# Two chained cross-attentions on one core: block 0 of pass 2 reordered on all engines, layer 1's softmax maxima by groups of 8 heads, and the last block's second spread moved between its outputs

## The chip, the core and the metric

The kernel runs on one core of one Trainium2 chip. The metric is the device time in microseconds (us), lower is better. A core has TensorE (PE, matrix products), VectorE (DVE), ScalarE (ACT) and GpSimd (POOL); SyncE (SP) issues the DMAs. Matrix products write to 8 PSUM banks of 128 x 512 f32. POOL works on SBUF alone.

## The reference

x is 2 x 2048 x 512, the context 2 x 128 x 512, and the mask is over context positions. Two layers follow each other:

```
layer 0 (16 heads of 64):  A = exp(mask*(Q K') - max over all) * mask;  A /= sum(A) + 1e-15
                           y = layernorm((A V) Wo + bo + x) * gamma + beta
layer 1 (16 heads of 32):  A = softmax(Q K' / sqrt(32)), queries from y, keys and values from the context
                           out = layernorm((A V) Wo + bo + y) * gamma + beta
```

## The kernel before

The 4096 query rows are 8 blocks (`i`, `NB` = 8) of 512 rows; a block has 4 tiles (`n`) of 128 rows. Dense products are made of three products of high and low parts (`split_product`, lines 408 to 411), so there is a `*_hi` (ACT) and a `*_lo` (POOL or DVE) version of each operand. A "step" below is one chunk `c` of such a product: 3 matrix products of 128 x 512.

**Pass 1** makes layer 0's attention for all blocks and stores it unscaled (`u_dram`) with its row sums. Its end is `values0(NB - 1, j)`, j = 0 to 3, each behind `mask_probs` of DVE; two banks hold its results, which ACT copies out (`save_u`), so chunk c waits until chunk c - 2 is saved.

**Pass 2** runs blocks 0 to 7. Each engine has an order written out by hand, and semaphores (`wait_ge`) tie the engines. For block i:

- `attention0(i, n)` (POOL) scales `a_raw` by the reciprocal sums `r_bc`, which come back from DRAM (`store_r`, then `load_r`); for block 0 DVE does it (`attention_first`). `a0_high` (ACT) and `a0_low` (POOL) split it, and `output0(i, n)` (PE, 8 steps, `Z_BANKS[n % 2]`) multiplies it by Wo.
- `rows0`, `statistics0`, `moments0` (DVE), `scales0` (POOL, half a block) and `normal0` (ACT) are the layernorm; `transposes` (PE), `yt_high` (ACT), `yt_low` (DVE) give yt.
- `queries1(i, c)` (PE, 4 steps), `q1_high` (ACT), `q1_low` (DVE) and `logits1(i, c)` (PE, 4 heads, one per `L_BANKS`) follow; `scores_and_max1` (DVE, per head) copies the logits out and takes row maxima into `mx1`.
- **The maxima over rows.** `max_row1` (PE) transposes the maxima of a group of heads, `head_max` (DVE) reduces them, `max_spread1` (PE) sends the result to all partitions, `shift1` (DVE) turns it into the bias of `exponential1` (ACT, per head). A group is 4 heads, four groups to a block, in `MAX1_BANKS` (the two `Z_BANKS` and `L_BANKS[0]`). Groups 1 to 3 fall among the first two `output0` tiles of the next block.
- `sums1(i, c)`, `values1(i, c)` (PE), `divisors1` (DVE: `den1`, reciprocal, cast to `r1_hi`, `r1_split`), `spread1` (PE), `save_u1` (ACT), `attention1` (DVE), `a1_high` (ACT), `a1_low` (POOL) give layer 1's attention inside block i + 1; `output1`, `rows1`, `statistics1`, `moments1`, `scales1`, `normal1`, `out_scale`, `out_bias` the rest.

ACT at the start of block i + 1 has the remaining `exponential1(i, h)`, `normal0(i + 1, 0)`, `normal0(i + 1, 1)`, `a0_high(i + 2, 0)`, `save_u1`, `a0_high(i + 2, 1)`, `a1_high`. POOL there has `scales0(i + 1, 0)`, then `attention0` and `a0_low` of block i + 2 for tiles 0 and 1, then `a1_low(i, c)`, then `scales0(i + 1, 1)`.

**Block 0** prepares layer 1's weights too: PE's `value_product` for v1 and 32 small products for the bias bq1, DVE's `wq1_lo` and `wo1_lo`. On DVE `wo1_lo` stands ahead of `rows0(0, 3)` and waits for `r_stored` of all blocks, since its source lies where another buffer is being stored from. On POOL, `scales0(0, 1)` stands behind `attention0(1, 0)` and `attention0(1, 1)`.

**The last block** has no next one: `divisors1` is done in two halves, and for each half PE makes four `spread_last`, then two `output1` tiles. The half's `attention1`, `a1_high` and `a1_low` lie between the spreads and the outputs. DVE adds, normalizes and scales tiles 1 to 3 (`rows1`, `statistics1`, `moments1`, lines 1259 and 1263).

## Time and profile before

| what | value |
|---|---|
| median of 3 runs | 934.73 us (931.45 to 936.63) |
| the profiled execution's own time | 935.43 us |
| its span, first to last instruction | 933.6 us |
| mean granted TensorE clock | 0.972 of 2.4 GHz |
| busy: PE, DVE, ACT, POOL | 875.1, 552.8, 419.6, 454.2 us |
| pass 2 starts near | 387 us |
| one block of pass 2, from one block's first `sums1` to the next one's | 61.7 us |

The span is the time between the first and the last instruction; the run's own time has 1.8 us more. Busy time of PE counts modelled ends of pipelined products, so steps are read from start to start. A line such as L409 is a line of the program.

### The profile page before, as it was taken

Reading aid. Unit: us, or ns where it says so; the run is one execution under the profiler, and the core shown is the slowest. Engines: PE = TensorE matmul, PEld = TensorE weight load, DVE = VectorE, ACT = ScalarE, POOL = GpSimd, SP = SyncE. Lnnn points to the kernel's source line nnn. Section 1 sums busy time; section 2 is a strip of 40 time slices with the busy share of each in tenths; the row PEclk is TensorE's granted clock in tenths of the full one; section 3 lists DMA queues with packets and bytes.
Section 4 is the critical chain, followed back from the end, with each engine's and each line's share of the span. In section 5 each row is a group of like instructions: output and inputs, shape, how many; then the busy total and the mean of one; then the engine's idle time right before and its main releaser. Section 6 shows DMA issues by size and latency. Waiting matters only on the chain.

```text
span 933.6 us, 12121 instructions
## 1 busy us (share of the span) xinstructions
PE 875.1 (94%) x4556; PEld 588.2 (63%) x4556; DVE 552.8 (59%) x1080; ACT 419.6 (45%) x560; POOL 454.2 (49%) x284
## 2 busy tenths in 40 slices
PE   7989999999999989794999999999999999999964
PEld 6567466574756654473667687686776876767633
DVE  1357575665656577835666566555665665556645
ACT  2325374553536437323453644536545454363440
POOL 0510312303031113428388579586795786853714
PEclk9999999999999999896999999999999999999977
DMA  9622416152452426971341431523414224210011
GB/s 351 230 81 111 168 70 225 62 194 91 149 194 59 182 92 222 275 212 40 96 128 48 136 91 50 177 68 100 149 46 135 91 76 151 68 69 1 1 46 45
DMA packets 47641, 111.55 MB, mean 119 GB/s; under 512 B 4704, under 2 KB 8544, under 8 KB 47584
## 3 DMA queue, kind: packets, MB, share of 16 engines
q1 hardware_dynamic: 47584, 110.78, 35.9%
q8 instruction: 36, 0.59, 0.3%
q14 instruction: 21, 0.17, 0.1%
HBM read 76.69 MB, written 34.08 MB: 119 GB/s over the span
## 4 chain that ended last, share of the span: by engine, by line
PE 70%; DVE 11%; POOL 7%; DMA 4%; issue 4%; ACT 3%; SPq 1%; POOLq 0%; DVEq 0%
PE bank L409 15%; PE bank L411 14%; PE bank L410 14%; PE bank L457 6%; PE bank L469 6%; PE bank L450 5%; PE bank L616 2%; DVE den L1101 2%; PE bank L574 2%; DVE scores L1084 2%; PE bank L397 2%; POOL a_lo L1308 2%; POOL a_raw L1298 2%; PE bank L403 1%; POOL resid L1370 1%
## 5 line engine op out<-in xcount | busy, mean ns | idle before, releaser
L409 PE MATMUL bank<-wo_lo,a_hi 128*128 128x512 f32 x384 | 157.0, 409 | 10.8 <-POOL a_lo L1423 6.9
L1270 POOL TENSOR_TENSOR x_lo<-x_raw,x_hi 128x2048 fp32r<-128x2048 f32 x8 | 39.0, 4876 | 235.1 <-ACT x_hi L758 235.1
L411 PE MATMUL bank<-wo_hi,a_hi 128*128 128x512 f32 x384 | 151.6, 395 | 0.0
L410 PE MATMUL bank<-wo_hi,a_lo 128*128 128x512 f32 x384 | 151.6, 395 | 0.0
L970 DVE CUSTOM_DVE_ANT_0 scores<-bank,mask_f 128x512 f32<-128x512 f32 x128 | 80.8, 687 | 58.1 <-PE bank L450 58.1
L846 ACT ACTIVATE scores<-scores,sh 128x512 f32<-128x512 f32 x128 | 82.0, 712 | 56.3 <-DVE sh L1094 56.2
L409 PE MATMUL bank<-x_lo,wq_hi 128*128 128x512 f32 x256 | 103.0, 402 | 4.3 <-DVE q_lo L961 3.5
L1303 POOL TENSOR_TENSOR a_lo<-a_raw,a_hi 128x1024 fp32r<-128x1024 f32 x32 | 78.4, 2453 | 50.1 <-ACT a_hi L827 50.1
L411 PE MATMUL bank<-x_hi,wq_hi 128*128 128x512 f32 x256 | 100.6, 393 | 0.0
L410 PE MATMUL bank<-x_hi,wq_lo 128*128 128x512 f32 x256 | 100.6, 393 | 0.0
L768 ACT ACTIVATE q_hi<-bank,bq_sb 128x512 fp32r<-128x512 f32 x64 | 44.1, 689 | 116.8 <-PE bank L411 114.0
L409 PEld LDWEIGHTS bank<-wo_lo,a_hi 128*128 128x128 f32 x384 | 73.2, 191 | 35.9 <-issue 10.8
L1084 DVE TENSOR_SCALAR_CACHE_REDUCE scores<-bank 128x512 f32<-128x512 f32 x128 | 81.9, 680 | 6.3 <-PE bank L574 5.7
L411 PEld LDWEIGHTS bank<-wo_hi,a_hi 128*128 128x128 f32 x384 | 73.2, 191 | 16.1
L410 PEld LDWEIGHTS bank<-wo_hi,a_lo 128*128 128x128 f32 x384 | 73.4, 191 | 13.9
L994 DVE TENSOR_TENSOR scores<-scores,mask_f 128x2048 f32<-128x2048 f32 x32 | 77.2, 2416 | 0.0
L961 DVE SCALAR_TENSOR_TENSOR q_lo<-bank,bq_sb,q_hi 128x512 fp32r<-128x512 f32 x64 | 47.9, 749 | 49.1 <-ACT q_hi L768 48.6
L1298 POOL TENSOR_TENSOR a_raw<-a_raw,r_bc 128x1024 f32<-128x1024 f32 x28 | 69.5, 2481 | 11.3 <-DMA r_bc<-r_dram 11.3
L827 ACT ACTIVATE a_hi<-a_raw 128x1024 fp32r<-128x1024 f32 x32 | 33.9, 1060 | 77.1 <-POOL a_raw L1298 71.3
L469 PE MATMUL bank<-scores,v 128*64 128x512 f32 x256 | 63.7, 620 | 4.8 <-ACT u_out L790 4.7
L457 PE MATMUL bank<-scores,summer 128*32 128x512 f32 x512 | 67.0, 618 | 0.0
L774 ACT ACTIVATE scores<-scores,neg_mx 128x2048 f32<-128x2048 f32 x32 | 64.1, 2002 | 0.0
(134 smaller groups left out, 1602.4 us busy)
## 6 DMA issues: line engine op xcount, KB each, us to landing
u_dram<-u_out SPq DMA_DIRECT2D x8, 2048.0 KB, 7.4
a_raw<-u_dram SPq DMA_DIRECT2D x32, 512.0 KB, 3.6
r_bc<-r_dram SPq DMA_DIRECT2D x56, 256.0 KB, 4.9
x_raw<-x_t SPq DMA_DIRECT2D x8, 1024.0 KB, 5.5
xn<-x_n SPq DMA_DIRECT2D x8, 1024.0 KB, 5.1
xb_dram<-xn SPq DMA_DIRECT2D x8, 1024.0 KB, 5.2
z<-xb_dram SPq DMA_DIRECT2D x32, 256.0 KB, 2.8
out<-z SPq DMA_DIRECT2D x7, 1024.0 KB, 6.8
```

What stands on the lines that cost most here:

```text
L409: nc.tensor.matmul(dst, lh, rl, start=first, stop=False)
L410: nc.tensor.matmul(dst, ll, rh, start=False, stop=False)
L411: return nc.tensor.matmul(dst, lh, rh, start=False, stop=last)
L457: last = nc.tensor.matmul(dst[32 * g:32 * g + 32, :], summer[:, j, :], scores[:, G * j + g, :], start=(j == 0), stop=(j == HG - 1))
L469: last = nc.tensor.matmul(U_BANKS[c % 2][a * DK0:(a + 1) * DK0, :], v0[:, b, h * DK0:(h + 1) * DK0], scores[:, h, :], start=True, stop=True)
L774: nc.scalar.activation(four, four, ACT.Exp, bias=neg_mx[:]).then_inc(exp_ready, 1)
L846: nc.scalar.activation(scores[:, h, :], scores[:, h, :], ACT.Exp, bias=sh1[:, h:h + 1], scale=SCALE1).then_inc(probs1_ready, 1)
L970: nc.vector.tensor_tensor_reduce(out=scores[:, h, :], in0=L0_BANKS[h % 4][:], in1=mask_f[:], scale=1.0, scalar=-3e38, op0=ALU.mult, op1=AL ...
L994: nc.vector.tensor_tensor(four, four, mask_f[:].unsqueeze(1).to_broadcast([P, HG, QB]), ALU.mult).then_inc(probs_ready, 1)
L1084: nc.vector.tensor_scalar(scores[:, h, :], L_BANKS[h % HC1][:], 1.0, -3e38, ALU.mult, ALU.max, accum_out=mx1[:, h:h + 1]).then_inc(scores1 ...
L1298: nc.gpsimd.tensor_tensor(a_raw[:, n, :], a_raw[:, n, :], r_bc[:, n % 2, :], ALU.mult).then_inc(attn0_ready, 1)
L1303: nc.gpsimd.tensor_tensor(a_lo[:, n, :], a_raw[:, n, :], f(a_hi[:, n, :]), ALU.subtract).then_inc(a0_ready, 1)
```

## The change

**Maxima (blocks 0 to 6).** Two groups of 8 heads in place of four of 4, in `TQ_BANKS[0]`, which is free at that time, so that `output0` of the next block no longer waits for `shift1`:

```diff
-        MAX1_BANKS = [Z_BANKS[0], Z_BANKS[1], Z_BANKS[1], L_BANKS[0]]
+        MAX1_BANK = TQ_BANKS[0]
+        def max_groups(i):
+            return [(0, 8), (8, 16)] if i < NB - 1 else [(0, 8), (8, 12), (12, 16)]
...
+                    elif i == 1:
+                        pe.wait_ge(z0_ready, n + 3)
                     else:
-                        pe.wait_ge(shift1_ready, C1 * (i - 1) + (1 if n == 0 else 3))
+                        pe.wait_ge(z1_ready, QT * (i - 2) + n + 3)
...
+                if g == 0:
+                    pe.wait_ge(q1_ready, C1 * i + 3)
+                else:
+                    pe.wait_ge(shift1_ready, N_MAX * i + g)
+                pe.wait_ge(scores1_ready, H1 * i + last)
```

PE's order at the start of a block, and from `queries1(i, 2)` on:

```diff
             for i in range(NB):
                 before = i > 0
-                output0(i, 0, 0, C0 // 2)
+                output0(i, 0, C0 // 2 if before else 0)
+                output0(i, 1, 0, 1)
+                if before:
+                    logits1(i - 1, 3)
+                output0(i, 1, 1, 6)
+                if before:
+                    max_row1(i - 1, 1)
+                output0(i, 1, 6)
                 if before:
                     max_spread1(i - 1, 1)
-                    logits1(i - 1, 3)
-                    max_row1(i - 1, 2)
-                output0(i, 0, C0 // 2)
-                if before:
-                    max_spread1(i - 1, 2)
-                output0(i, 1, 0, C0 // 2)
-                if before:
-                    max_row1(i - 1, 3)
-                output0(i, 1, C0 // 2)
-                if before:
-                    max_spread1(i - 1, 3)
...
                 queries1(i, 2)
+                if i + 1 < NB:
+                    output0(i + 1, 0, 0, 1)
                 logits1(i, 1)
+                queries1(i, 3)
+                if i + 1 < NB:
+                    output0(i + 1, 0, 1, 2)
                 max_row1(i, 0)
-                queries1(i, 3)
+                if i + 1 < NB:
+                    output0(i + 1, 0, 2, 4)
                 max_spread1(i, 0)
                 logits1(i, 2)
-                max_row1(i, 1)
```

Behind the last spread `sums1` and `values1` now come as sums 0, 1, values 0, 1, sums 2, values 2, sums 3, values 3. ACT does 8 exponentials at the end of a block and 8 at the start of the next (before: 4 and 12). DVE:

```diff
                 if before:
-                    shift1(i - 1, 1)
-                    scores_and_max1(i - 1, H1 - 4)
-                    scores_and_max1(i - 1, H1 - 3)
-                    head_max(i - 1, 2)
-                    scores_and_max1(i - 1, H1 - 2)
-                    scores_and_max1(i - 1, H1 - 1)
-                    shift1(i - 1, 2)
+                    for h in heads(C1 - 1):
+                        scores_and_max1(i - 1, h)
                 rows0(i, 0)
                 statistics0(i, 0)
                 moments0(i, 0)
                 if before:
-                    head_max(i - 1, 3)
-                    shift1(i - 1, 3)
+                    head_max(i - 1, 1)
+                    shift1(i - 1, 1)
                 rows0(i, 1)
```

**Block 0.** PE: `value_product` for the first batch moves from behind `transposes(0, 1)` to behind `values0(NB - 1, 3)`; the 32 products for bq1 move from ahead of `transposes(0, 2)` to behind `transposes(0, 3)`; `queries1(0, 0)` waits for `wq1_lo` and no longer for `wo1_lo` and bq1. ACT, ahead of its loop:

```diff
-            for n in range(2):
-                save_u(NB - 1, 2 * n + 2, 2 * n + 4)
-                a0_high(0, n)
+            save_u(NB - 1, 2, 6)
+            a0_high(0, 0)
             save_u(NB - 1, 6)
+            a0_high(0, 1)
             a0_high(0, 2)
             a0_high(0, 3)
```

In ACT's block 0 `a0_high(1, 0)`, formerly behind `normal0(0, 1)`, comes behind `normal0(0, 3)`; `a0_high(1, 1)`, from there too, behind `yt_high(0, 3)`; `a0_high(1, 2)` and `a0_high(1, 3)` behind `q1_high(0, 1)` and `q1_high(0, 2)`. DVE: `k1_low(2)` and `k1_low(3)` move ahead of `attention_first(0)`; `wo1_lo` with its waits moves from ahead of `rows0(0, 3)` to behind `q1_low(0, 0)`; bq1's copy to behind `yt_low(0, 3)`. POOL:

```diff
                 scales0(i, 0)
+                if not before:
+                    scales0(i, 1)
                 if more:
                     for n in (0, 1):
                         attention0(i + 1, n)
```

**Last block.** Its maxima are three groups (8, 4 and 4 heads), with `sums1(7, 0)` and `sums1(7, 1)` among them, and:

```diff
-            for half in range(2):
-                for c in range(C1):
-                    spread_last(half, c)
-                output1(i, 2 * half)
-                output1(i, 2 * half + 1)
+            for c in range(C1):
+                spread_last(0, c)
+            output1(i, 0)
+            for c in range(C1):
+                spread_last(1, c)
+            for n in range(1, QT):
+                output1(i, n)
```

## Rows read from the trace of the kernel before

**Rows 1.** The page, busy time by engine.

```profile
PE 875.1 (94%) x4556; PEld 588.2 (63%) x4556; DVE 552.8 (59%) x1080; ACT 419.6 (45%) x560; POOL 454.2 (49%) x284
```

**Rows 2.** PE's waits: line, releaser: us in total, times, longest.

```profile
PE bank L546 <- ACT z L831: 9.7, 1, 9.7
...
PE bank L469 <- ACT u_out L790: 4.7, 1, 4.7
```

**Rows 3.** Windows: stretch, length, busy of PE, PEld, DVE, ACT, POOL, PEclk, DMA share, GB/s.

```profile
378.00:387.00 9.00, 5.38 (x17) 1.11 (x17) 7.25 (x6) 4.28 (x6) 5.93 (x2) 0.62 1.01 268
420.00:439.00 19.00, 6.39 (x23) 5.11 (x23) 11.35 (x15) 6.63 (x9) 15.25 (x10) 0.55 0.18 51
884.00:893.00 9.00, 7.38 (x35) 2.85 (x36) 4.69 (x19) 6.64 (x11) 4.48 (x2) 0.62 0.30 115
```

**Rows 4.** Timeline of block 0, by engine: start, us, engine, line [idle before, releaser].

```profile
379.94 1.06 ACT L827 ACTIVATE a_hi<-a_raw 128x1024 fp32r<-128x1024 f32 x1 [5.73 <-DVE a_raw L1028]
...
381.07 6.45 POOL L1303 TENSOR_TENSOR a_lo<-a_raw,a_hi 128x1024 fp32r<-128x1024 f32 x2 [16.11 <-ACT a_hi L827]
...
397.11 0.62 DVE L1060 TENSOR_TENSOR z<-bank,z 128x512 f32<-128x512 f32 x1
...
409.76 7.03 PE L403 MATMUL bank<-wv_sb,ctx_sb 128*128 128x512 f32 x16
416.63 3.63 PE L695 MATMUL bank<-b_col,s_stage 128*128 128x1 f32 x32
...
413.26 2.35 POOL L1298 TENSOR_TENSOR a_raw<-a_raw,r_bc 128x1024 f32<-128x1024 f32 x1 [11.30 <-DMA r_bc<-r_dram]
...
418.54 2.73 DVE L1173 TENSOR_TENSOR wo_lo<-s_stage,wo_hi 128x2048 fp32r<-128x2048 f32 x1 [13.19 <-DMA r_dram<-den]
...
427.48 4.84 DVE L1187 SCALAR_TENSOR_TENSOR wq_lo<-s_stage,g_col,wq_hi 128x512 fp32r<-128x512 f32 x4
...
434.81 0.76 PE L409 MATMUL bank<-yt_lo,wq_hi 128*128 128x512 f32 x1 [2.93 <-DVE yt_lo L1073]
```

**Rows 5.** Timeline, PE, one block's maxima: queries1, queries1, logits1, max_row1, sums1.

```profile
556.91 0.39 PE L409 MATMUL bank<-yt_lo,wq_hi 128*128 128x512 f32 x1
...
562.35 0.39 PE L409 MATMUL bank<-yt_lo,wq_hi 128*128 128x512 f32 x1
...
569.00 0.73 PE L574 MATMUL bank<-q_lo,k_hi 32*128 32x512 f32 x4
...
585.60 0.27 PE L589 MATMUL bank<-ident,mx 128*4 128x128 f32 x1
...
588.84 2.78 PE L457 MATMUL bank<-scores,summer 128*32 128x512 f32 x24
```

**Rows 6.** Timeline, the stretch behind those sums, ACT, POOL, DVE and PE.

```profile
589.15 2.56 ACT L846 ACTIVATE scores<-scores,sh 128x512 f32<-128x512 f32 x4 [3.90 <-DVE sh L1094]
...
595.80 2.42 POOL L1303 TENSOR_TENSOR a_lo<-a_raw,a_hi 128x1024 fp32r<-128x1024 f32 x1 [1.17 <-ACT a_hi L827]
598.16 2.40 POOL L1298 TENSOR_TENSOR a_raw<-a_raw,r_bc 128x1024 f32<-128x1024 f32 x1
...
599.24 1.60 DVE L1105 CAST r_hi<-den 128x512 fp32r<-128x512 f32 x1
...
609.45 0.50 PE L409 MATMUL bank<-wo_lo,a_hi 128*128 128x512 f32 x1 [0.15 <-POOL a_lo L1308]
```

**Rows 7.** Timeline, DVE, the same cast in block 7.

```profile
846.00 0.43 DVE L1105 CAST r_hi<-den 128x512 fp32r<-128x512 f32 x1
```

**Rows 8.** Timeline, the last block's outputs and spreads (PE), then statistics of tile 2 (DVE).

```profile
905.53 0.80 PE L409 MATMUL bank<-wo_lo,a_hi 128*128 128x512 f32 x1 [3.45 <-POOL a_lo L1423]
...
912.73 0.64 PE L637 MATMUL bank<-r_split,hs 128*128 128x256 f32 x4
916.83 0.79 PE L409 MATMUL bank<-wo_lo,a_hi 128*128 128x512 f32 x1 [3.46 <-POOL a_lo L1423]
...
923.08 0.69 DVE L1128 BATCH_NORM_STATS2 st<-z 128x6 f32<-128x512 f32 x1
```

More of the change, by code:

```diff
@@ L142, in cross_attention_program, with group_of @@
         SUM1_BANK = TQ_BANKS[1]
-        MAX1_BANKS = [Z_BANKS[0], Z_BANKS[1], Z_BANKS[1], L_BANKS[0]]
-        def max1_bank(i, c):
-            return Z_BANKS[0] if i == NB - 1 and c == C1 - 1 else MAX1_BANKS[c]
+        MAX1_BANK = TQ_BANKS[0]
+        def max_groups(i):
+            return [(0, 8), (8, 16)] if i < NB - 1 else [(0, 8), (8, 12), (12, 16)]
+        def group_of(i, h):
+            return [h < last for first, last in max_groups(i)].index(True)
+        N_MAX = len(max_groups(0))
         LAST_BANKS = [[*TQ_BANKS, *Z_BANKS], [*TQ_BANKS, *L_BANKS[0:2]]]
@@ L640, in output1 @@
             def output1(i, n):
+                if i == 0 and n == 0:
+                    pe.wait_ge(wo1_ready, 1)
                 if n == 0:
@@ L687, in _ @@
                 if i == 0:
-                    for b in range(B):
-                        pe.wait_ge(*((kv1_done, C1) if b == 0 else (u_saved, (C0 + 1) * NB)))
-                        value_product(L_BANKS[b], wv1_sb, b, 0).then_inc(kv1_psum_ready, 1)
+                    pe.wait_ge(u_saved, (C0 + 1) * NB)
+                    value_product(L_BANKS[1], wv1_sb, 1, 0).then_inc(kv1_psum_ready, 1)
+                if before:
+                    output1(i - 1, 0)
+                    output1(i - 1, 1)
+                transposes(i, 2)
+                transposes(i, 3)
+                if i == 0:
                     pe.wait_ge(w1_loaded, 32)
@@ L698, in _ @@
                     last.then_inc(bq1_psum_ready, 1)
-                if before:
-                    output1(i - 1, 0)
-                    output1(i - 1, 1)
-                transposes(i, 2)
-                transposes(i, 3)
-                if i == 0:
-                    pe.wait_ge(w1_ready, 2)
-                    pe.wait_ge(bq1_ready, 1)
+                    pe.wait_ge(wq1_ready, 1)
                 if before:
@@ L881, in _ @@
                 if before:
-                    for c in range(1, C1):
-                        for h in heads(c):
-                            exponential1(i - 1, h)
+                    for h in range(H1 // 2, H1):
+                        exponential1(i - 1, h)
                 else:
@@ L894, in _ @@
                 normal0(i, 1)
-                if more:
-                    a0_high(i + 1, 0)
                 if before:
+                    if more:
+                        a0_high(i + 1, 0)
                     for c in range(C1):
                         save_u1(i - 1, c)
-                if more:
-                    a0_high(i + 1, 1)
-                if before:
+                    if more:
+                        a0_high(i + 1, 1)
                     for c in range(C1):
@@ L908, in _ @@
                 normal0(i, 3)
-                if more:
+                if before and more:
                     a0_high(i + 1, 2)
+                if i == 0:
+                    a0_high(1, 0)
                 yt_high(i, 2)
                 yt_high(i, 3)
-                if more:
+                if before and more:
                     a0_high(i + 1, 3)
                 if i == 0:
+                    a0_high(1, 1)
                     act.wait_ge(bq1_ready, 1)
@@ L921, in _ @@
                     normal1(i - 1, 1)
+                else:
+                    a0_high(1, 2)
                 q1_high(i, 2)
@@ L925, in _ @@
                     normal1(i - 1, 3)
+                else:
+                    a0_high(1, 3)
                 q1_high(i, 3)
-                for h in heads(0):
+                for h in range(H1 // 2):
                     exponential1(i, h)
             i = NB - 1
-            for c in range(1, C1):
-                for h in heads(c):
-                    exponential1(i, h)
+            for h in range(H1 // 2, H1):
+                exponential1(i, h)
             for c in range(C1):
```

125 lines of the change are left out of this document (59 added, 66 removed).

## The prediction

> **What bounds the kernel now.** I began with busy time: PE has 94% of the span and no other engine is above 59% [rows 1], so PE sets the pace, and a change is worth what it takes out of PE's own queue: products, idle time, and time at the half clock. Next I read PE's waits. The longest is 9.7 us at `transposes(0, 2)`, for ACT's `normal0`; another of 4.7 us stands at the end of `values0(7, j)`, for ACT's `save_u` [rows 2], and one of 2.9 us at `queries1(0, 0)` [rows 4]. All three lie in block 0. The third view is the windows: around these waits the granted clock averages 0.62 and 0.55 [rows 3], so stretches run at 1.2 GHz instead of 2.4. At 0.62 over 9 us, (1 - 0.62) x 9 / 0.5 = 6.8 us were at the half clock. Such a spell costs up to 3.4 us of products. Last I read one regular block on PE [rows 5] and the other engines behind its sums [rows 6]: PE is busy nearly without a gap, but it reaches `output1` 0.15 us before POOL's `a1_low`. That chain is so tight that what it loses PE loses.
>
> **Block 0, part by part.** *ACT's `save_u`.* ACT stood 5.7 us in `a0_high(0, 0)` until DVE's product at 379.9 [rows 4], with the saves that PE needed behind it. Now the saves of chunks 4 and 5 come first, and `values0(7, 3)` needs only these. The 4.7 us go, the half clock of 378 to 387 [rows 3] goes with its cause, and the sums are done near 379.7 instead of 387. The moved `value_product` fills what follows: a pair of batches took 409.76 to 416.63 [rows 4], so one is 3.4 us, to 383.2. `k1_low(2)` and `(3)`, on which it waits, move into DVE's idle time ahead of `attention_first(0)`, at nothing; behind it they would have held the product to 382.7. `output0(0, 0)` then waits for `a0_low(0, 0)`: ACT's `a_hi` at 379.94 has not moved, and two `a_lo` from 381.07 take 6.45 us [rows 4], so the first is there at 384.4.
>
> *The four output tiles.* A step costs 3 x 0.2267 us: one chunk of queries and one `output1` tile, 24 products, take 562.35 - 556.91 = 5.44 us [rows 5]. A tile of 8 steps is then 5.44 us. Tile 1 ends at 395.3. Tile 2 needs `rows0(0, 0)`, which DVE reached at 397.11 [rows 4] behind its divisors, whose order and covers don't change: it starts at 397.8, a new wait of 2.4 us. Tile 3 ends at 408.7, much as before (near 409). So the time that the first part frees is eaten here but for the value product that is already done.
>
> *Behind them.* Two transposes (0.9), the second value product (3.4) to 413.1. Meanwhile DVE no longer stands in `wo1_lo`, which waited 13.2 us for a store until 418.54 [rows 4]; `rows0(0, 3)`, its statistics and moments are done 1.9 us behind tile 3 (two of 0.7, the rest small), at 410.6. POOL does `scales0(0, 1)` at once (1.4 us), and `normal0(0, 2)`, `(0, 3)` follow to 413.7: the transposes go nearly without waiting, where they waited 9.7 us. The 32 bq1 products take 3.6 us [rows 4], to 417.9. DVE's four `wq1_lo` take 4.84 us [rows 4]; behind the copy of v1 they run from 413.8 to 418.6. `a0_high(1, 0)` stands ahead of `yt_high(0, 2)` on ACT, so yt hangs on POOL's `attention0(1, 0)`. That was held until 413.26 by `r_bc` [rows 4]; SP's stores and loads ahead of it were held by the late sums and start some 5 us earlier, so I take it from 412.1, behind `scales0`, to 414.5. With `a_hi` and two `yt_high` to 416.7 this is hidden behind `wq1_lo`; the two `yt_low` end at 419.9. `queries1(0, 0)` starts at 419.9 after a wait of 2.0 us, against 434.81 [rows 4]: 14.9 us earlier. The two first queries took 7.1 us there (to 441.9) because of the clock of rows 3, and take 5.5 now: 1.6 more. `wo1_lo` stands ahead of `q1_low(0, 1)` at about 424.4; what it waits for is there by 418.5 even if it doesn't move. Its 2.73 us [rows 4] hold `q1_low(0, 1)` and the first `scores_and_max1`, and behind them PE's `logits1(0, 1)`, which comes 3.6 us later anyway, at 430; I charge 0.5. ACT's `a0_high(1, 1)` to `(1, 3)` stand among `q1_high`; by the same count they are ready when reached. Block 0 gives 16.0 us to the start of `queries1(0, 2)`.
>
> I take back 3.0 us for the clock. In 884 to 893 PE idled 1.6 of 9 us, in short waits, and 6.8 us of it ran at the half clock all the same [rows 3]; the new waits of 2.4 and 2.0 us may bring one (cost 0 to 6.8 for none to two). Net 13.0, between 8 and 17.
>
> **The maxima.** From `queries1(i, 1)` at 562.35 to `sums1(i, 0)` at 588.84 the trace has 26.5 us [rows 5]. In it are 84 products of 0.2267 us (19.0) and four `logits1`. One `logits1` costs 569.00 - 562.35 - 5.44 = 1.21 us, breaks of both sides included, so 4.8. The remaining 2.6 us are four transposes, four spreads and their waits. One transpose with one spread costs 588.84 - 585.60 - 2.72 = 0.52 us between its steps, 0.6 with the break ahead. Two pairs are 1.2 us, so a block gains 1.4 us, and the seven blocks 0 to 6 gain 9.8. A transpose to 8 rows and a reduction over them have no row here; both move the same 128 columns as with 4, so I take the same, and at most twice (0.3 us each), which on DVE is idle time; a cheaper one is not excluded but worth as little. The new waits of `output0` (z1 or z0 of older tiles) and `max_row1(i, 0)` (`q1_low(i, 2)`) are met some us before.
>
> **What it costs behind the sums.** ACT used to have 4 exponentials behind the last shift, 589.15 for 2.56 us [rows 6]; now it has 8, 5.2 us. With S the start of `sums1(i, 0)` (588.84), they end at S + 5.55, where `sums1(i, 3)`, after six groups of 0.86 us, would start at S + 5.2: 0.4 us of wait. Queued behind them are `normal0` (1.5) and `a0_high(i + 2, 0)` (1.1), so that POOL's `a0_low`, at 595.80 or S + 7.0 before, starts at S + 8.05. `attention0(i + 2, 1)`, from 598.16 or S + 9.3, then runs from S + 10.4 to S + 12.8. All of POOL's queue to `a1_low(i, 3)` shifts by 1.1. There is a second path. DVE's cast took 1.60 us at 599.24 and ended 0.3 us after POOL's 598.16 + 2.40; in block 7, with no `attention0` beside it, 0.43 us [rows 6, 7]. Its start moves by the 0.4 to S + 10.8, POOL's product by 1.1 to S + 10.4, so it waits 2 us, and `r1_split` is out at S + 13.95, where PE is ready at S + 13.2. Both paths bring `output1(i, 0)` to S + 21.8 against 609.45, S + 20.6: 1.2 us lost in each of the six blocks 1 to 6, 7.2 in all (between 0.4 a block, only the exponentials, and 1.8, the second path with both waits in series). The block behind the last of these has no `attention0` and loses 0.4.
>
> The Trainium skill (SBUF — State Buffer, "Who interferes with whom") states that a VectorE cast in a two-port mode and a GpSimd instruction exclude each other, and that whoever starts first holds the ports for its whole instruction. The 1.60 and 0.43 us agree. By the rule the cast gets nothing until POOL's product ends, as in the sum; were the ports shared, this path would vanish and the POOL queue alone would still give 1.1.
>
> **The last block.** With ACT and DVE doing the same work in larger groups, its last `values1` ends 1.5 us earlier (between 0 and 2): one group less, and sums between the transposes. Then the second spreads. Before, two output tiles from 905.53 took 7.2 us, and only then came the spreads at 912.73, whose chain over DVE, ACT and POOL lasted 4.1 us, 3.46 of them idle on PE [rows 8]. Now the spreads come after one tile, at 910.0 (the first 3.7 us at the half clock), and the second tile, 2.7 us, covers the chain: `output1(7, 2)` starts at 914.1, 2.7 us earlier, with 0.6 us idle, and without that wait I expect no spell behind it. DVE then sets the end: behind its second half at 911.8 it has two tiles' sums and statistics and the scaling of tile 1, and reaches the statistics of tile 2 at 918.8, against 923.08 [rows 8]. All behind it follows as it did: 4.2 us (between 2.5 and 6).
>
> **The sum**, against the profiled execution's 935.4 us: block 0 -13.0; maxima -9.8; behind the sums +7.2 + 0.4; last block -1.5 and -4.2. Together -20.9: **914.5 us**. Its span would be 912.7. That execution is 0.7 us above the median of the runs, so the median expected is 914.
>
> **Rivals.** *The maxima gain in full and no spell comes.* For it: POOL has 49% [rows 1], and the new gaps are short. Against: the 0.15 us at `output1` [rows 6]. It gives 914.5 - 6 x 1.2 - 3 = 904.
>
> *Block 0's gain is held back on ACT.* `a0_high(1, n)` among `q1_high` makes PE's queries wait for POOL's products, and these exclude DVE's `wq1_lo` and `wo1_lo` if the cast shows a general thing. If they cost each other twice the 2.4 us of a product, the queries end 5 to 6 us later: 920.
>
> *The clock falls in every block; this is the one on the other side.* In place of PE waiting 0.35 us at a shift, each interval now has a wait of 0.4 us and one of 0.8 us, 8 us apart. For it: the spell of 884 to 893, among short waits [rows 3]. Against: waits of this size alone, in the regular blocks, brought none. One spell per block costs 6 x 3.4 = 20.4 us: 935, no gain; with two, 955. It decides the sign from six spells on.
>
> *The reordering does nothing, the DMA chain behind `r_bc` binds.* Then `attention0(1, 0)` stays at 413.3, 1.2 us behind my count. That moves little, so this one is inside the forecast.
>
> **How the numbers follow.** Forecast 0.52, with 909 to 919 as its own range; full gain 0.17; held back 0.18; the clock 0.06, half of it slower than before; what I can't name 0.07, of which 0.02 within 0.5%. A measurement of this kernel can tell about 0.5% (4.7 us) from no change. Faster (below 930) 0.92, within 0.05, slower 0.03. The range of 903 to 923 leaves out the clock and the worst of the rest. The predicted time is 914.
>
> **What would show it.** PE's waits of 9.7 and 4.7 us gone, new ones of 1.2, 2.4 and 2.0 us near 383, 395 and 418, with the releasers `a_lo`, z of DVE and `yt_lo`; first `queries1` near 420 to 423. In regular blocks 25.1 us from `queries1(i, 1)` to the sums, then a wait of 0.4 us for an exponential and 0.8 us for `r_split` or 1 us for `a_lo` of L1308, the cast at 2 us or more, and a period of 61.5 us (61.7 - 1.4 + 1.2), hardly less than before. At the end one wait of 0.6 in place of 3.46. Wrong would make me: `queries1(0, 0)` after 428, a period below 60.5 or above 62.5, or the clock below 1.0 in blocks 2 to 6.

## The result, and the profile after

The changed kernel takes 912.06 us (median of 4 runs, 909.61 to 914.73) against 933.09 us (4 runs, 930.63 to 936.63): a ratio of 0.975, 95% interval 0.9722 to 0.9778. Forecast were 914.0 us and 903 to 923. The profiled execution is one of the quick ones: 909.97 us, span 908.2 against 933.6.

Busy time of PE after, to [rows 1], and the list of its waits, to [rows 2] (line, releaser: us in total, times, longest):

```profile
PE 861.4 (95%) x4511; PEld 577.5 (64%) x4511; DVE 553.0 (61%) x1050; ACT 416.2 (46%) x560; POOL 456.1 (50%) x284
```

```profile
PE bank L636 <- DVE r_split L1129: 5.6, 6, 2.2
...
PE bank L600 <- DVE scores L1104: 3.6, 2, 2.7
...
PE bank L416 <- DVE z L1080: 2.4, 1, 2.4
...
PE bank L416 <- DVE yt_lo L1093: 1.4, 1, 1.4
...
PE bank L416 <- POOL a_lo L1318: 1.0, 6, 0.2
```

The 9.7 us for ACT's z and the 4.7 us for `u_out` are gone. New are one wait of 2.4 and one of 1.4 us in block 0, six for `r_split`, six small ones for `a_lo`, and two at the transposes of the maxima.

To place the difference I cut both spans at the same eight points on PE: the first product of layer 1's keys (k1), the first `queries1`, the first `sums1` of each block (S0 to S6), the last `values1`, the last block's first `output1`. The fourth column is one more profiled execution of the changed kernel (span 913.3, experiment 12); the last is my sum, put on the same stretches.

| stretch, us | before | changed | changed, again | predicted difference |
|---|---|---|---|---|
| start to k1 | 359.4 | 357.2 | 360.6 | 0 |
| k1 to first `queries1` | 75.4 | 60.3 | 59.1 | } -13.0 - 1.4 |
| to S0 | 30.6 | 29.2 | 30.1 | } |
| S0 to S1 | 61.7 | 62.2 | 64.3 | -0.2 |
| S1 to S6, five blocks | 308.5 | 302.3 | 302.2 | -1.0 |
| S6 to the last `values1` | 61.9 | 63.6 | 63.6 | +0.4 - 1.5 |
| to `output1(7, 0)` | 8.0 | 8.2 | 8.2 | 0 |
| to the end | 28.1 | 25.2 | 25.2 | -4.2 |

Between the medians the sum was right (21.0 us measured, 20.9 forecast); behind k1 the two profiles differ from the kernel before by 23.2 and 21.5 us. Its terms were not right. Block 0 gave 16.6 and 16.9, not 14.4; the regular blocks 6.2, not 1.0; two stretches that should have gained or stayed lost 0.5 to 2.6 and 1.7; the end gave 2.9, not 4.2. The first line is no effect of the change: before it PE's work is the same, and in the profile of before 3.4 us at the half clock lie in it, near 336, which the first profile of the changed kernel lacks. A regular block (S1 to S2 and on) repeats within 0.1 us between executions. Block 0 doesn't: nine executions that leave it as the change has it (this profile and numbers 4 to 9, 11 and 12) took 59.0 to 63.6 us from k1 to the first `queries1`, with a median of 60.3, and S0 to S1 moves by several us too. So the experiments are read by stretch, and in block 0 a single execution shows only what lies outside this scatter.

Block 0 after, to [rows 4] (start, us, engine, line; idle before, releaser):

```profile
394.76 0.47 PE L416 MATMUL bank<-wo_lo,a_hi 128*128 128x512 f32 x1 [2.45 <-DVE z L1080]
...
417.53 0.77 PE L416 MATMUL bank<-yt_lo,wq_hi 128*128 128x512 f32 x1 [1.40 <-DVE yt_lo L1093]
```

```profile
409.20 2.36 POOL L1308 TENSOR_TENSOR a_raw<-a_raw,r_bc 128x1024 f32<-128x1024 f32 x1
```

```profile
410.88 5.31 DVE L1195 SCALAR_TENSOR_TENSOR wq_lo<-s_stage,g_col,wq_hi 128x512 fp32r<-128x512 f32 x4
...
423.41 3.05 DVE L1223 TENSOR_TENSOR wo_lo<-s_stage,wo_hi 128x2048 fp32r<-128x2048 f32 x1
```

PE and POOL of a regular block, to [rows 5] and [rows 6], and PE of the last block's outputs, to [rows 8]:

```profile
484.48 0.39 PE L416 MATMUL bank<-yt_lo,wq_hi 128*128 128x512 f32 x1
...
508.89 1.07 PE L464 MATMUL bank<-scores,summer 128*32 128x512 f32 x8
...
514.26 0.64 PE L464 MATMUL bank<-scores,summer 128*32 128x512 f32 x4
...
522.53 0.73 PE L636 MATMUL bank<-r_split,hs 128*128 128x512 f32 x2 [0.68 <-DVE r_split L1129]
...
530.31 0.50 PE L416 MATMUL bank<-wo_lo,a_hi 128*128 128x512 f32 x1 [0.17 <-POOL a_lo L1318]
```

```profile
509.20 5.01 ACT L862 ACTIVATE scores<-scores,sh 128x512 f32<-128x512 f32 x8 [5.73 <-DVE sh L1116]
```

```profile
882.99 0.80 PE L416 MATMUL bank<-wo_lo,a_hi 128*128 128x512 f32 x1 [3.18 <-POOL a_lo L1435]
...
892.38 0.50 PE L416 MATMUL bank<-wo_lo,a_hi 128*128 128x512 f32 x1 [0.76 <-POOL a_lo L1435]
```

From `queries1(2, 1)` to the sums it is 508.89 - 484.48 = 24.4 us, where [rows 5] have 26.5; from the sums to `output1` 530.31 - 508.89 = 21.4 against 20.6. In block 0, the wait for `rows0(0, 0)` is the 2.4 us forecast; `queries1(0, 0)` comes 60.3 us behind k1 (60.5 forecast); `attention0(1, 0)` stands right behind `scales0(0, 1)` with no wait for `r_bc`; `wo1_lo` doesn't wait any more. The 1.2 us for `a0_low` near 383 did not come in this profile, as the attention tiles were about 1 us earlier against k1; in numbers 3, 4, 7, 9 and 11 a wait of 0.65 to 1.6 us for it stands there.

### The profile page after: what moved, and what is told of

It reads as the page before. It is cut to its first block, busy times and chain, and to the rows that moved or that the text cites. A ratio compares the mean times of both kernels' runs of the same rounds, so it can differ in the third digit from the quotient of the medians.

```text
span 908.2 us, 11986 instructions
## 1 busy us (share of the span) xinstructions
PE 861.4 (95%) x4511; PEld 577.5 (64%) x4511; DVE 553.0 (61%) x1050; ACT 416.2 (46%) x560; POOL 456.1 (50%) x284
## 4 chain that ended last, share of the span: by engine, by line
PE 81%; DVE 11%; POOL 3%; issue 2%; DMA 2%; ACT 1%; SPq 0%; POOLq 0%; DVEq 0%
PE bank L416 18%; PE bank L417 17%; PE bank L418 16%; PE bank L464 6%; PE bank L476 6%; PE bank L457 5%; PE bank L586 3%; PE bank L626 3%; DVE den L1123 2%; PE bank L410 2%; PE bank L404 2%; POOL a_lo L1318 2%; DVE r_hi L1127 1%; DMA r_first<-r_dram 1%; DVE scores L1014 1%
## 5 line engine op out<-in xcount | busy, mean ns | idle before, releaser
L418 PEld LDWEIGHTS bank<-wo_hi,a_hi 128*128 128x128 f32 x384 | 72.7, 189 | 15.7
L417 PEld LDWEIGHTS bank<-wo_hi,a_lo 128*128 128x128 f32 x384 | 72.8, 190 | 13.7
L1308 POOL TENSOR_TENSOR a_raw<-a_raw,r_bc 128x1024 f32<-128x1024 f32 x28 | 67.6, 2415 | 2.6 <-DMA r_bc<-r_dram 2.6
L806 ACT ACTIVATE u_out<-bank 128x512 f32<-128x512 f32 x64 | 37.2, 596 | 58.2 <-PE bank L476 58.2
```

Of the source, the lines that this page charges most:

```text
L417: nc.tensor.matmul(dst, ll, rh, start=False, stop=False)
L418: return nc.tensor.matmul(dst, lh, rh, start=False, stop=last)
L1308: nc.gpsimd.tensor_tensor(a_raw[:, n, :], a_raw[:, n, :], r_bc[:, n % 2, :], ALU.mult).then_inc(attn0_ready, 1)
```

## The experiments

All but number 12 are the changed kernel with one edit (number 3 moves ScalarE's casts along with it, number 11 joins two edits). The kernel before ran beside them at 934.36 us (1 to 8) and 933.83 us (median of 9; 9 to 12). Numbers 1 to 10 are one execution each.

### 1. The saves in their old order

```diff
-            save_u(NB - 1, 2, 6)
+            save_u(NB - 1, 2, 4)
             a0_high(0, 0)
-            save_u(NB - 1, 6)
+            save_u(NB - 1, 4, 6)
             a0_high(0, 1)
+            save_u(NB - 1, 6)
```

> Changed kernel with ScalarE's saves of the last sums of pass 1 and the first two a_hi casts back in their old order (a save pair, a cast, a save pair, a cast, the rest). Theory (the order of the saves is a large part of what block 0 gained): the cast a_hi of tile 0 waits for its attention tile with saves 4 to 7 queued behind it, the value products and the first output0 start 3 to 5 us later, and the stretch from the first k1 product to the first queries1 grows from 60.3 to 63 to 66 us. Rival (TensorE's queue there is long enough, or the changed kernel's earlier attention tiles already feed the cast in time): the stretch grows by less than 1 us.

Measured: 914.23 us. A wait of 4.2 us for `u_out` is back, the first `output0` starts 29.3 us behind k1 instead of 23.9, and the first `queries1` 63.2 instead of 60.3. The theory holds for the wait and for `output0`, which started 23.4 to 25.6 us behind k1 in the nine executions with the changed block 0. The wait of 2.4 for `rows0(0, 0)` disappears in exchange, so of the 5.4 us lost ahead of `output0` only a part can arrive at the queries. How much isn't shown: against the first profile it is 2.9 us, but 63.2 lies inside the scatter of 59.0 to 63.6.

### 2. `wo1_lo` back ahead of `rows0(0, 3)`

```diff
                 moments0(i, 2)
+                if i == 0:
+                    dve.wait_ge(r_stored, 16 * NB)
...
+                                            ALU.subtract).then_inc(wo1_ready, 1)
                 rows0(i, 3)
```

> Changed kernel with VectorE's wo1_lo (3.0 us, and its four waits) back ahead of rows0(0,3). Theory (its waits on the stores and the casts held VectorE there and everything behind it came late): the stretch from the first k1 product to the first queries1 grows from 60.3 to 65 to 67 us, by the 3.0 us of the operation and its wait for ScalarE's wo1_hi, and the wait behind it is named by rows0(0,3). Rival (weight casts by ScalarE end first and the wq1_lo group waits anyway): it grows by the 3.0 us of the operation at most.

Measured: 917.58 us, first `queries1` 67.4 us behind k1. VectorE's row says what it cost (start, us; idle before, releaser):

```profile
412.32 2.29 DVE L1189 TENSOR_TENSOR wo_lo<-s_stage,wo_hi 128x2048 fp32r<-128x2048 f32 x1 [7.99 <-DMA r_dram<-den]
```

It is the store of `den` for which it waits, not ScalarE's cast as I had written in the expectation. `rows0(0, 3)` follows at 414.52, and PE waits 6.4 us for the normalised z. The edit costs 7.1 us against the first profile, 3.8 to 8.4 against the scatter of block 0.

### 3. `scales0(0, 1)` and the casts of block 1 where they were

```diff
                 scales0(i, 0)
-                if not before:
-                    scales0(i, 1)
...
                     for c in range(C1):
                         a1_low(i - 1, c)
-                    scales0(i, 1)
+                scales0(i, 1)
```

ScalarE's `a0_high(1, n)` go back to the places of the other blocks with it; one without the other would deadlock.

> Changed kernel with GpSimd's scales0(0,1) back behind attention tiles 0 and 1 of block 1 and their a_lo, and with ScalarE's a_hi casts of block 1 where the other blocks have them. Theory (the normalisation of tiles 2 and 3 waits for GpSimd): yt of tiles 2 and 3 come 10 us or more later, the first queries1 comes 8 to 11 us later, stretch 68 to 71 us. Rival (the weight operations of block 0 on VectorE, wq1_lo 5.3 us, are the bound there): under 4 us later, stretch under 64 us.

Measured: 923.18 us, first `queries1` 74.2 us behind k1, where 68 to 71 were expected: 13.9 us of the 15.1 are gone with this edit alone (10.5 to 15.1 against the scatter). PE's row of tile 2's transposes:

```profile
425.22 1.94 PE L558 MATMUL bank<-ident,z 128*128 128x128 f32 x8 [9.45 <-ACT z L847]
```

That is the 9.7 us of [rows 2] again. The waits of numbers 2 and 3 (6.4 and 9.45 us) stand at the same transposes, and for the same z of ACT: the edits are gates ahead of the same products, and the one that opens last sets the time. So their costs don't add up (2.9 + 7.1 + 13.9 against the first profile is more than 15.1).

### 4. The last block's second spreads behind `output1(7, 1)`

```diff
-            for c in range(C1):
-                spread_last(0, c)
-            output1(i, 0)
-            for c in range(C1):
-                spread_last(1, c)
-            for n in range(1, QT):
-                output1(i, n)
+            for half in range(2):
+                for c in range(C1):
+                    spread_last(half, c)
+                output1(i, 2 * half)
+                output1(i, 2 * half + 1)
```

> Changed kernel with the last block's second set of spreads back behind output1(7,1). Theory: the stretch from output1(7,0) to the end of the span was 28.1 before and 25.2 with the change; it goes back to 28 or more (plus 2.5 to 3.5). Rival (what was gained there is one clock spell less, not the order): it stays within 1 us of 25.2, or a half-clock spell is seen in one of the two and not in the other.

Measured: 913.16 us; from `output1(7, 0)` to the end 28.4 us instead of 25.2, and the idle 3.46 us of [rows 8] is back as 3.46:

```profile
895.44 0.50 PE L416 MATMUL bank<-wo_lo,a_hi 128*128 128x512 f32 x1 [3.46 <-POOL a_lo L1433]
```

The order is worth 3.2 us here. 2.7 of them are idle time (3.46 against 0.76); the rest isn't split, since 3.4 us at the half clock followed this wait (from 895.8) and none stood there in the changed kernel, which is what the rival said one would see. As the idle time itself is back, the rival can't be the whole.

### 5 and 6. How many groups of maxima

Number 5: four groups of four in every block, in the one bank, with products of `output0` still between. Number 6: groups of 8, 4 and 4 in every block.

```diff
-            return [(0, 8), (8, 16)] if i < NB - 1 else [(0, 8), (8, 12), (12, 16)]
+            return [(0, 8), (8, 12), (12, 16)]
...
                 output0(i, 0, C0 // 2 if before else 0)
+                if before:
+                    max_row1(i - 1, 1)
                 output0(i, 1, 0, 1)
                 if before:
+                    max_spread1(i - 1, 1)
                     logits1(i - 1, 3)
```

> Changed kernel with the maxima of layer 1 in four groups of four heads again, in every block, but still in their one bank and with the products of the next block's output0 between row and spread as the changed kernel has them. Theory A (what the blocks gained is the number of breaks: two rows and two spreads fewer, about 0.15 to 0.6 each with their waits): the steady period between first sums goes from 60.45 to 61.5 to 62.5, at or above the 61.7 of the kernel before. Rival B (the gain is that every row and spread now stands behind other work, whatever their number): the period stays under 61.0. For the last block, where nothing stands between: A none changed or slower; B the 2.7 us wait of the second row for VectorE's scores is gone, and with it the half clock that follows it.

> Changed kernel with groups of 8, 4 and 4 heads in every block, as its last block has them: four exponentials instead of eight stand behind the last shift. Theory (ScalarE's eight exponentials behind the last shift are what makes the r_split wait of 0.7 and moves the sums by 0.2): the waits for r_split and a_lo in a steady block (0.68 and 0.17) go, and one more row and spread costs 0.2 to 0.3: period 59.8 to 60.2 against 60.45. Rival (r_split is late through its own chain behind the sums on VectorE, the cast blocked by GpSimd above all, and not through the exponentials): the wait stays at 0.5 or more and the period is 60.5 to 60.8.

Measured, for a regular block, with the number of groups (us):

| kernel | first `queries1` to sums | sums to next `queries1` | period |
|---|---|---|---|
| before (4, three banks) | 31.9 | 29.8 | 61.7 |
| 5 (4, one bank) | 31.6 | 29.8 | 61.4 |
| 6 (3) | 30.2 | 29.8 | 60.0 |
| changed (2) | 29.85 | 30.6 | 60.45 |

Totals 916.61 and 910.87 us. Number 5's period lies 0.1 below theory A's range, and far from the rival's 61.0. The theory of number 6 holds for the period and for `r_split`; the wait of 0.16 us for `a_lo` stays. Two groups fewer are worth 1.75 us ahead of the sums, but not in equal parts: from four to three 1.4, from three to two 0.35. The new bank and places are worth 0.3. Behind the sums the changed kernel pays 0.8, and all of that comes from the eight exponentials behind the last shift: with four, the wait for `r_split` is gone. In the last block number 5 has no 2.7 us at the second row any more, as rival B said, and is yet only 0.6 us shorter than the changed kernel from its queries to its last `values1` (33.4 against 33.9); number 8 takes that up.

### 7. The divisors in PSUM

```diff
-                nc.vector.tensor_scalar(den1[:], SUM1_BANK[:], 1e-36, None, ALU.max).then_inc(den1_ready, 1)
+                nc.vector.tensor_scalar(SUM1_BANK[:], SUM1_BANK[:], 1e-36, None, ALU.max).then_inc(den1_ready, 1)
...
-                nc.vector.tensor_copy(r1_hi[:], den1[:]).then_inc(r1_hi_ready, 1)
+                nc.vector.tensor_copy(r1_hi[:], SUM1_BANK[:]).then_inc(r1_hi_ready, 1)
```

The reciprocal and the split read and write the bank likewise.

> Changed kernel whose divisors of blocks 0 to 6 stay in their PSUM bank through the maximum, the reciprocal, the cast and the split, instead of den1 in SBUF. Theory (the cast at 2.2 us where 0.43 is its time elsewhere, and the r_split of 2.7 us in block 0, are VectorE locked out by GpSimd's attention0 while it reads SBUF in its fast form): cast takes 0.5 to 0.8, r_split 0.7 to 0.9, the wait of the first spread for r_split goes from 0.68 to under 0.2 in steady blocks and from 2.17 to under 1 in the first; as GpSimd's a_lo is the next to end, the steady period falls by 0.2 to 0.7, the first one (62.2) by 1 to 2. Rival (the cast waits for something else, a read of the same bank or the PE's values): its time stays near 2 us and the period does not move by more than 0.1.

First the same stretch in the changed kernel, block 2 (the other side of [rows 6]), then in number 7, each DVE and POOL:

```profile
519.51 2.18 DVE L1127 CAST r_hi<-den 128x512 fp32r<-128x512 f32 x1
```

```profile
519.01 2.40 POOL L1308 TENSOR_TENSOR a_raw<-a_raw,r_bc 128x1024 f32<-128x1024 f32 x1
```

```profile
528.50 0.69 DVE L1127 CAST r_hi<-bank 128x512 fp32r<-128x512 f32 x1
529.22 0.75 DVE L1129 SCALAR_TENSOR_TENSOR r_split<-r_hi,low_rows,bank 128x512 fp32r<-128x512 f32 x1
```

```profile
527.97 2.42 POOL L1308 TENSOR_TENSOR a_raw<-a_raw,r_bc 128x1024 f32<-128x1024 f32 x1
```

With `den1` in SBUF the cast ends 0.3 us behind GpSimd's product (519.01 + 2.40 = 521.41, and 521.69); with the source in PSUM it takes 0.69 us with the same product beside it. In SBUF alone it takes 0.43 [rows 7]. So the exclusion is of SBUF reads, as the theory said, and PE's wait for `r_split` is gone in all blocks. The period falls by 0.25 only, to 60.2: `output1` now waits 0.8 for `a_lo`, POOL's queue. Both paths of the prediction are real and nearly equal: with both, `queries1` comes 0.8 us later behind the sums than in number 6, with POOL's alone 0.6.

The part on the first interval was wrong: 65.45 us, and the whole 917.92. There `r_bc` came 3.2 us late, POOL's queue became the bound with all of that, and the clock fell (0.89 granted over the 30 us from 460).

### 8. Four groups in the last block alone

Edit as in number 5, for `i == NB - 1` only, rows and spreads in the order of before.

> Changed kernel with only its last block's maxima in four groups of four heads, in the old order (row 1 covers heads 4 to 7, which are done when it is asked for). Theory (three groups make TensorE wait 2.7 us for the scores of heads 8 to 11 at the second row, and the clock falls there): no wait over 0.5 at the second row, the stretch from the last block's first queries1 to its first sums 23.9 as before or less against 23.0 to 23.6, but the stretch from the first sums to the last values at full clock, 8.6 against 10.4 in the changed kernel; together 0 to 1.5 shorter. Rival (the clock falls there for other reasons, and the later waits for scores only move): 8.6 to 11.7 as in the runs so far, and the sum of both not shorter.

The changed kernel's last block first (PE), and the windows over its sums (columns as in [rows 3]):

```profile
861.62 0.37 PE L600 MATMUL bank<-ident,mx 128*4 128x128 f32 x1 [2.72 <-DVE scores L1104]
...
867.15 0.37 PE L600 MATMUL bank<-ident,mx 128*4 128x128 f32 x1 [0.85 <-DVE scores L1104]
```

```profile
861.00:871.00 10.00, 8.16 (x42) 2.81 (x46) 3.89 (x14) 6.01 (x11) 3.24 (x2) 0.50 0.28 107
```

Measured for number 8: 909.30 us. The 2.7 us at the second row are gone, and 1.2, 0.9 and smaller waits for `top` stand at its spreads instead.

| last block, us | first `queries1` to sums | sums to last `values1` | together |
|---|---|---|---|
| before | 23.85 | 8.6 | 32.4 |
| 8 (4 groups) | 24.8 | 8.4 | 33.2 |
| changed; 12; 9; 10; 11 (3 groups) | 23.5 | 10.2 to 10.9 | 33.8 to 34.4 |
| 1; 2; 7 (3 groups) | 22.9 to 23.5 | 11.6 to 11.75 | 34.6 to 35.3 |
| 3; 4; 6 (3 groups) | 23.0 to 23.35 | 8.6 | 31.6 to 32.0 |

The eleven executions with three groups have the same order of work there and the same 2.7 us of wait. In all eleven a spell of the half clock begins near the end of this wait, from 1.7 us ahead of it to 1.3 us behind it. In three of them it lasts 3.4 us and covers the first 1.6 to 2.4 us of the sums, the values run at full clock, and the stretch is 0.5 to 0.8 us shorter than before (where 3.0 us of the sums were at the half clock); in eight it lasts 10.2 or 13.7 us and lies over sums and values, and the stretch is 1.4 to 2.9 longer. With four groups it came out between, with a spell of 6.8 us that began 0.4 us behind the wait of 1.2 and covered 2.7 us of the sums. Number 8's first stretch, 24.8 us, is longer than its theory allowed (23.9), and the whole 0.7 shorter than in the changed kernel. So the loss is the clock; that the 2.7 us bring it is likely from where it falls, but as number 8 is a single execution and part of the clock is lost there as well, it isn't shown. What decides how long the spell lasts stays open.

### 9. `r_bc` ahead of the z loads

```diff
                     for n in (0, 1):
                         load_u(i + 1, n)
-                        load_r(i + 1, n)
+                        if i == 0:
+                            load_r(1, n)
...
+                    if i + 2 < NB:
+                        for n in (0, 1):
+                            load_r(i + 2, n)
                     for n in range(QT):
                         load_xb(i + 1, n)
```

> Changed kernel in which SyncE's queue issues the broadcast loads of r_bc for tiles 0 and 1 of block i+2 before the four z loads of block i+1, instead of behind them and each behind its own a_raw load. In the changed kernel GpSimd's first attention0 of block 2 waits 2.56 us for r_bc, and the second one then lies over VectorE's cast and r_split: the interval from the first sums of block 0 to those of block 1 is 62.2 (61.0 to 65.5 in the runs so far) against 60.45 in the others. Theory (the late r_bc makes all of it): no wait for r_bc there, r_split 0.75, the first interval 60.4 to 60.7, the other intervals unchanged within 0.05. Rival (the a_raw load is as late as r_bc, since its issue stands behind the z loads as well): the wait only changes its name, and the interval stays above 61.3.

In the changed kernel (SyncE's queue, POOL, DVE, PE), whose S0 is at 446.69:

```profile
437.13 5.65 SPq L333 DMA_DIRECT2D z<-xb_dram  x4
442.84 0.42 SPq L319 DMA_DIRECT2D a_raw<-u_dram  x1
443.31 1.09 SPq L325 DMA_DIRECT2D r_bc<-r_dram  x2
```

```profile
452.77 2.39 POOL L1308 TENSOR_TENSOR a_raw<-a_raw,r_bc 128x1024 f32<-128x1024 f32 x1 [2.56 <-DMA r_bc<-r_dram]
...
458.68 2.54 POOL L1308 TENSOR_TENSOR a_raw<-a_raw,r_bc 128x1024 f32<-128x1024 f32 x1
```

```profile
459.04 2.73 DVE L1129 SCALAR_TENSOR_TENSOR r_split<-r_hi,low_rows,den 128x512 fp32r<-128x512 f32 x1
```

```profile
461.82 0.50 PE L636 MATMUL bank<-r_split,hs 128*128 128x512 f32 x1 [2.17 <-DVE r_split L1129]
```

And number 9, PE and POOL at the same place:

```profile
465.06 0.73 PE L640 MATMUL bank<-r_split,hs 128*128 128x512 f32 x2 [0.68 <-DVE r_split L1133]
```

```profile
454.89 2.39 POOL L1312 TENSOR_TENSOR a_raw<-a_raw,r_bc 128x1024 f32<-128x1024 f32 x1
```

The read is a chain of four engines: GpSimd's `resid_scale(0, 1)` (439.52 to 441.92) holds the last z load, the `r_bc` load behind it is issued 3.4 us ahead of S0, right behind five others, `attention0(2, 0)` waits for `r_bc`, the next one comes to lie over VectorE's `r_split`, and PE waits 2.2 us where regular blocks wait 0.7. In number 9 S0 to S1 takes 60.45 us, as every other block, and the waits have the regular block's sizes. The theory holds in full, and the other executions with two groups and no spell of the half clock in this interval say the same, with the cast and the split as the changed kernel has them:

| number | wait of `attention0(2, 0)` for `r_bc` | S0 to S1 |
|---|---|---|
| 9; 3 | none | 60.45; 60.5 |
| 4 | 1.36 | 61.0 |
| 2 | 1.45 | 61.1 |
| 8 | 2.07 | 61.7 |
| changed | 2.56 | 62.2 |

About 0.8 us of the wait is absorbed, and the rest comes out one for one. Number 3 has no wait even without the edit of number 9, likely because its block 0 is nearly as long as before. The whole of number 9, 912.44, shows less of the gain, because k1 to the first `queries1` took 62.6 us there, with 3.4 us more at the half clock near 400 and a wait of 0.65 for `a0_low`.

### 10. The attention tiles ahead of `k1_low(2)` and `(3)`

```diff
+            attention_first(0)
+            attention_first(1)
             k1_low(2)
             k1_low(3)
-            attention_first(0)
-            attention_first(1)
             attention_first(2)
```

> Changed kernel with VectorE's first two attention tiles ahead of its last two k1_lo subtractions again, as before the change. Theory (the attention tiles wait for the r_first transfers, not for VectorE, and k1_lo behind them held back the value product that the change puts in front of output0): the first output0 starts 23.9 to 25 after the first k1 product (23.9 in the changed kernel) and the first queries1 0 to 1 later than 60.3. Rival (k1_lo behind the attention tiles is on the chain to everything in block 0): both 2 us or more later.

Measured: 913.63 us. PE waits 1.9 us for `k_lo` ahead of the value product, the first `output0` comes 25.4 behind k1 (1.5 later than in the first profile, 0.4 beyond the theory's range, but inside the scatter of 23.4 to 25.6), the first `queries1` at 60.2, not later at all: the wait of 2.4 for z shrinks to 0.5. So the 1.9 us at `k_lo` are paid back at z. The rival is excluded, and the move is worth nothing as long as `rows0(0, 0)` stands behind the divisors.

### 11 and 12. Three groups and early `r_bc`, beside the changed kernel

Number 11 joins the edits of 6 and 9; number 12 is the changed kernel as it is.

> The version to which the runs so far point: three groups of maxima in every block (8, 4 and 4 heads) and the broadcast loads of r_bc ahead of the z loads. Theory: steady period 60.0 (as with three groups alone, 0.44 under the changed kernel's), the first interval 60.0 to 60.3 instead of 62.2 (64.4 with three groups alone), the last block as in the changed kernel; 2.5 to 4.5 us under the changed kernel on the same chip: 907 to 910, ratio to the kernel before 0.970 to 0.974. Rival (what the first interval gets back is lost to a later wait for the a_raw loads): within 1.5 us of the changed kernel.

> The changed kernel itself, unaltered, on the same chip and between the same runs of the kernel before as the combined version, for a direct comparison: 910 to 915 us, ratio 0.972 to 0.978. Its profile shows by how much the stretches of one and the same kernel differ between executions: steady period 60.45 within 0.05, block 0 within 3 us by the clock, the first interval 61 to 63, the stretch from the last block's first sums to its last values 8.6 at full clock or 10.4 to 11.8 with the half clock.

| | median, us | runs | ratio to before, 95% |
|---|---|---|---|
| 11 | 909.31 | 4, 906.37 to 911.26 | 0.9737, 0.9714 to 0.976 |
| 12 | 913.05 | 5, 910.25 to 915.09 | 0.9773, 0.9754 to 0.9793 |

Number 11 is 3.7 us under the changed kernel, as its theory said; the two intervals overlap by a little (0.9754 to 0.976), so the totals alone don't settle it. Its profile has 60.1 us from S0 to S1 (64.3 in number 12) and 60.0 in each regular block (60.45), as expected. Number 12's S0 to S1 is outside the 61 to 63 expected. The wait for `r_bc` was 3.35 us there, 0.8 more than in the first profile, and 3.4 us of the interval ran at the half clock; the other 1.3 of the 2.1 us more are likely that spell: numbers 1 and 10, with one of the same length, lie 1.4 and 1.3 us above what the table of number 9 gives for their waits (2.32 and 2.50).

## Why the prediction came out

The total came out where it was forecast, and partly by luck: errors of both signs met. One of the three signs by which the prediction would have called itself wrong did come, a period below 60.5 (60.45). The other two, a late `queries1(0, 0)` and a clock below 1.0 in blocks 2 to 6, did not.

**Block 0** was right by its steps. The saves, `wo1_lo` and `scales0` each hold a gate (numbers 1 to 3; for the saves the cost at the queries is not shown), the freed time is eaten by `rows0(0, 0)` (1 and 10), and the first `queries1` came within 0.2 us of the forecast in one execution and 1.4 earlier in the other. The one spell of the half clock that I took back 3.0 us for did come, 6.8 us at 1.2 GHz around the queries in one execution and 10.2 in the other. To `queries1(0, 2)` block 0 gave 15.2 and 15.0 us instead of 13.0. That is not proof that the spell was charged too high: over the nine executions with this block 0 the gain is 11.2 to 15.7 us, with a median of 13.8, against the one profile of before.

**"A block gains 1.4 us" (the maxima)** was mis-sized: 2.1. I counted a transpose with its spread at 0.6 us, and even so wrote 1.4 for two pairs, which make 1.2. Measured, the two pairs gave 1.75, but unequally (1.4 and 0.35, numbers 5 and 6), plus 0.3 for the bank and the places. One price per pair was the error.

**"1.2 us lost in each of the six blocks"** was mis-sized too: 0.8. The mechanism was right to the row: the exponentials end late (`sums1(i, 3)` at S + 5.37, 0.2 late and not 0.4), the cast is shut out by `attention0` until S + 12.5 and ends at S + 12.8, `r_split`'s spread waits 0.68 for 0.8 forecast, `a_lo` 0.17. The size failed in the first link: the eight exponentials took 5.01 us and ended at S + 5.3, not S + 5.55, and GpSimd's product starts at S + 10.1, not S + 10.4, which brings the spread to S + 13.6 instead of S + 13.95. POOL's own path, which I let arrive together with DVE's, is some 0.2 us ahead of it (number 7). The two errors, 0.7 and 0.4 us a block, go the same way, and are the 5.2 us by which the regular blocks beat the sum.

**"The reordering does nothing, the DMA chain behind `r_bc` binds"** I had placed at block 1's tiles and set inside the forecast. The chain bound one block later, at block 2's, which the prediction never looked at: 1.75 us and up to 3.85 where a spell came too (number 12), shown by number 9 and its table. In the kernel before, SyncE began to issue the z loads 21.8 us ahead of S0 and that `r_bc` 6.3 us ahead; in the changed one it is 9.6 and 3.4, both behind one another, since S0 comes 18.7 us earlier and GpSimd's `resid_scale`, which holds the last z load, only 6.4.

**"Its last `values1` ends 1.5 us earlier"** had the wrong sign: 1.5 us later. The step took the groups' count and left out that in the last block no other product stands between `logits1(7, 2)` and the row that needs its scores, 2.7 us idle, with the half clock behind it. Where the values kept the full clock the gain is 0.5 to 0.8 (number 8).

**"4.2 us" at the end** measured 2.9 (number 4: 3.2). Behind `output1(7, 0)` the statistics of tile 2 start after 14.6 us instead of 17.55; I had 13.3. VectorE's second half ended 0.7 us later than counted, as the first output tile had 5.2 us at the half clock and not 3.7. The scaling of tile 1 took 1.74 us where the last tile's takes 0.75. It took 1.73 in the kernel before too, so the profile had it; a product of GpSimd stands beside the first and none beside the second:

```profile
895.13 1.29 POOL L1440 TENSOR_TENSOR z<-z,g_b 128x512 f32<-128x512 f32 x1
...
895.24 1.74 DVE L1273 SCALAR_TENSOR_TENSOR z<-z,rs,be_b 128x512 f32<-128x512 f32 x1 [1.08 <-POOL rs L1359]
...
905.02 0.75 DVE L1273 SCALAR_TENSOR_TENSOR z<-z,rs,be_b 128x512 f32<-128x512 f32 x1 [0.79 <-POOL rs L1359]
```

The rivals: no spell in every block came (clock 1.00 in the regular blocks), and block 0 was not held back on ACT. The forecast of 914 held because errors met, which is luck: the regular blocks and block 0 gave 7.5 us more than their terms, and S0 to S1, the last block and the end 5 to 7 us less.

## What to carry to other kernels

When a long first stage is shortened, follow the transfers that used to hide in it into the next block, not only the first: a load issued behind others by program order became the next bound here. Grouping reductions trades breaks ahead of a point for work behind it; count both, and try the uneven split (8, 4, 4), which kept most of the one without the other. And judge parts by stretches between fixed points: a regular block repeats to 0.1 us, while the total of one execution moves by 5.

## What the hardware showed

- VectorE and GpSimd shut each other out, and where VectorE's operands lie decides it. The cast took 2.18 us from SBUF and 0.69 from PSUM beside the same GpSimd product. The `r_split` operation with two inputs in SBUF took 2.73 us beside one and 0.75 without, and 0.75 with one input in PSUM (number 7). The Trainium skill (SBUF — State Buffer, "Who interferes with whom") says that a VectorE instruction with two SBUF inputs contends with a GpSimd instruction that reads SBUF, and one with at most one such input outside the two-port modes doesn't; both halves agree. The prediction had used the rule for the cast only. GpSimd loses too: beside VectorE's four `wq1_lo` of block 0 its two operations of 2.4 us took 2.91 and 2.80 us.
- Around one and the same wait of 2.7 us on PE, in the last block, the granted clock fell to 0.50 in all eleven executions with that code there, for 3.4 us in three, 10.2 in six and 13.7 in two. In some it fell before the wait was over. In all thirteen executions with the changed block 0 or a variant of it, 6.8 us or more at the half clock stood around the first queries, though in eleven of them no wait in the 20 us ahead of them was over 2.5 us.
